# A two-layer graph network on one core: one-hots made in pairs, block transposes on VectorE in the late groups, and h0 remade by ScalarE

## The reference, cut to what matters

```python
h = jnp.maximum(_layernorm(x, axis=-1), 0.0)              # "h0"
# first layer
msg = h[src] + edge_attr_512
msg = msg @ Wm.T + bm
agg = segment_sum(msg, dst, 1250) / jnp.maximum(deg, 1.0)[:, None]
update = jnp.concatenate((h, agg), axis=-1) @ Wu.T + bu
out = h + gelu(update)
x = x + layernorm(out) * gamma + beta
# second layer
h = jnp.maximum(_layernorm(x, axis=-1), 0.0)              # "h1"
rst = (1.0 + eps[0]) * h + segment_sum(h[src], dst, 1250)
h2 = jnp.maximum(rst @ W1 + b1, 0.0) @ W2 + b2
x = x + h2 + h
```

## Time and profile before

| | |
|---|---|
| median of 3 runs | 529.69 us (528.18 to 530.55) |
| the profiled execution | 526.39 us, its span 524.6 us |
| TensorE busy in the span | 482.8 us (92%) |
| VectorE / ScalarE / GpSimd busy | 283.0 / 147.5 / 166.8 us |
| edge loads | 78 of 1024 KB and one of 128 KB, of 98.95 MB moved in all |
| mean granted TensorE clock | 0.992 |

### The profile page before, as it was taken

The page is one execution under the profiler, slowest core; times in us unless marked ns, Lnnn a source line. Parts: engine busy times, 40 slices in busy tenths (PEclk is TensorE's granted clock), DMA queues, the critical chain, the costliest instruction groups (busy, mean ns, idle before and its releaser), DMA issues.

```text
span 524.6 us, 8826 instructions
## 1 busy us (share of the span) xinstructions
PE 482.8 (92%) x3003; PEld 277.0 (53%) x3003; DVE 283.0 (54%) x660; ACT 147.5 (28%) x291; POOL 166.8 (32%) x217
## 2 busy tenths in 40 slices
PE   5889999898898988999999999599989999999997
PEld 4446554444444544675665655379944446744442
DVE  6897887888777779645434789983000000011111
ACT  4416644123222223222237245441011122100000
POOL 7323665333322224000023267636994000000000
PEclk9999999999999999999999999799999999999999
DMA  8998998889999999988820111112040000011111
GB/s 299 316 367 301 338 327 292 348 342 361 352 367 358 374 363 390 408 308 315 271 82 2 32 29 41 35 62 100 1 163 0 0 0 1 0 41 40 41 40 35
DMA packets 31115, 98.95 MB, mean 189 GB/s; under 512 B 3577, under 2 KB 3577, under 8 KB 31067
## 3 DMA queue, kind: packets, MB, share of 16 engines
q1 hardware_dynamic: 30458, 97.27, 50.7%
q10 hardware_dynamic: 608, 1.05, 0.7%
HBM read 95.76 MB, written 2.56 MB: 187 GB/s over the span
## 4 chain that ended last, share of the span: by engine, by line
PE 63%; DVE 21%; issue 6%; PEld 6%; DVEq 1%; POOL 1%; DMA 1%; SPq 0%; PEldq 0%; POOLq 0%
PE ps L1260 13%; PE ps L1245 13%; PE ps L1007 9%; PE ps L1048 7%; DVE A L669 5%; PE ps L1105 5%; PE ps L1106 4%; PE ps L1018 4%; PE ps L1194 3%; PEld ps L1171 3%; PE ps L1036 3%; PEld ps L1172 2%; DVE U L893 2%; DVE tt L871 2%; DVE oneS L648 2%
## 5 line engine op out<-in xcount | busy, mean ns | idle before, releaser
L400 POOL TENSOR_TENSOR aggT<-turned_sums,aggT 128x88 f32 x118 | 53.9, 456 | 107.4 <-ACT turned_sums L473 94.4
L1007 PE MATMUL ps<-ea,oneD 128*22 128x256 f32 x1264 | 83.9, 383 | 1.4 <-DVE oneD L640 0.9
L947 DVE TENSOR_TENSOR U<-ps,U 128x512 f32<-128x512 f32 (+1 forms) x10 | 6.9, 692 | 130.8 <-PE ps L1260 130.8
L467 ACT COPY packed_sums<-ps 128x256 f32<-128x256 f32 x79 | 29.4, 372 | 163.9 <-PE ps L1007 163.9
L1245 PE MATMUL ps<-aggT,W1s 128*128 (+1 forms) x192 | 67.4, 513 | 2.2 <-PEq L1239 2.2
L1260 PE MATMUL ps<-W2s,hid 128*128 128x512 f32 (+1 forms) x160 | 68.8, 592 | 0.0
L669 DVE TENSOR_TENSOR A<-ps,A 128x220 f32 x158 | 60.3, 381 | 8.6 <-PE ps L1018 8.0
L1018 PE MATMUL ps<-oneK,oneS 128*128 128x220 bf16 x316 | 42.5, 259 | 14.7 <-DVE oneS L648 13.0
L1245 PEld LDWEIGHTS ps<-aggT,W1s 128*128 128x128 f32 x192 | 36.4, 190 | 33.1 <-issue 33.0
L1007 PEld LDWEIGHTS ps<-ea,oneD 128*22 128x22 f32 x1264 | 30.5, 101 | 41.1 <-issue 23.6
L648 DVE TENSOR_TENSOR oneK<-iotaP,P_key 128x880 bf16<-128x880 bf16 x79 | 51.8, 655 | 0.0
(11 more groups left out here) (139 smaller groups left out, 645.1 us busy)
## 6 DMA issues: line engine op xcount, KB each, us to landing
ea<-in_edge_attr_dram SPq DMA_DIRECT2D x78, 1024.0 KB, 7.6
X<-in_x_dram SPq DMA_DIRECT2D x1, 2304.0 KB
xt<-in_x_dram SPq DMA_DIRECT2D x9, 256.0 KB, 2.7
out_dram<-U SPq DMA_DIRECT2D x9, 256.0 KB
W1s<-in_L_gnn_W_dram SPq DMA_DIRECT2D x1, 2048.0 KB, 7.7
W2s<-in_L_gnn_W_dram SPq DMA_DIRECT2D x1, 2048.0 KB, 8.7
WuN<-in_L_gnn_Wu_dram ACTq DMA_DIRECT2D x1, 1024.0 KB, 5.4
WuN<-in_L_gnn_Wu_dram SPq DMA_DIRECT2D x1, 1024.0 KB, 6.8
```

The lines of the kernel that those rows point to most:

```text
L400: nc.gpsimd.tensor_tensor(cols, sums, cols, ALU.add).then_inc(early_step, 1)
L1007: last = T.matmul(to.rearrange("p (c d) -> p c d", c=2), oneD[h][:, g * 2 + j, :], data, start=j == 0, stop=j == 1)
```

## The change

In the loop:

1. `oneK` and `oneS` are made for two groups by one instruction (`pair_hots`), with three buffers of two groups; `oneD` has three buffers and is made after the sums of the group before. The half of a group's one-hots that stood between and behind the two adds of `add_counts` is now one instruction between them: keys in even groups, sources in odd ones.
2. `u1(b)` is cut in two: two of its four matmuls in turn U_AT, two in the next.
3. From group 59 on sums are laid out by blocks of 32 columns (16 matmuls of 128 columns for 8 of 256), and VectorE transposes the 32 x 32 blocks straight out of PSUM (`turn_blocks`). The copy by ScalarE and TensorE's two transposes are gone for these 20 groups.
4. The low parts Hl, and the high parts with them, are made from turn 55 on and no longer in turns 6 to 17. A piece waits for its own low part alone.
5. The transposes of h0 stand in other turns, and the ten degree products stand one turn earlier, before `counts`.

In the normalisations: `h0t` is made by ScalarE from the loaded x (`h0_again`), beta is added by VectorE (`add_beta`), and GpSimd keeps the inverse roots alone. The late pieces stand one or two `map_agg` later.

```diff
-HOTS = 2
+HOTS = 3
+SUM_HOTS = 3
+TURNS = 2
...
-    T_AT = [4, 5, 6, 8, 9, 10, 11, 13, 14, 15]
-    U_AT = [7, 12, 16, 21, 26, 32, 37, 42, 47, 52]
-    HH_AT = [t + 2 for t in T_AT]
+    T_AT = [4, 5, 6, 10, 11, 15, 16, 20, 21, 25]
+    U_AT = [7, 12, 17, 22, 27, 32, 37, 42, 47, 52]
+    HH_AT = [FULL - 3 + b for b in range(NT)]
...
-            def ahead(b):
-                pool.wait_ge(xt_in[b % TB], 16 * (b // TB + 1))
-                nc.gpsimd.tensor_tensor(xt[b % TB][:], xt[b % TB][:], betaB[:], ALU.add).then_inc(xb_ready, 1)
-                if b >= TB:
-                    pool.wait_ge(o_sum, b - TB + 1)
-                nc.gpsimd.tensor_tensor(h0t[b % TB][:], Hh[:, b, :].bitcast(F32), Hl[:, b, :].bitcast(F32), ALU.add).then_inc(h0t_ready, 1)
...
+            def h0_again(b):
+                act.wait_ge(xt_in[b % TB], 16 * (b // TB + 1))
+                if b >= TB:
+                    act.wait_ge(o_sum, b - TB + 1)
+                nc.scalar.activation(h0t[b % TB][:], xt[b % TB][:], ACT.Relu, bias=nb0[:, b:b + 1], scale=rs0[:, b:b + 1]).then_inc(h0t_ready, 1)
...
             for k in range(NT + 4):
...
                 for work, lag in ((gelu, 0), (h1, 3), (h1_high, 3), (h1T, 3)):
                     if 0 <= k - lag < NT:
                         work(k - lag)
+                    if work is gelu and k + 1 < NT:
+                        h0_again(k + 1)
...
+            def pair_hots(p, hot, width, name, ready):
+                if p >= HOTS:
+                    dve.wait_ge(counts_done, 2 * (p - HOTS + 1))
...
+                V.tensor_tensor(hot[p % HOTS][:, 0:groups].rearrange("p g h c j -> p (g h) c j"), iota, mine, ALU.is_equal).then_inc(ready, 1)
...
+            def turn_blocks(n):
+                dve.wait_ge(sums_done, n + 1)
+                if n < TURNS + EARLY:
+                    dve.wait_ge(early_step, (n - TURNS + 1) * 2)
+                else:
+                    dve.wait_ge(sum_step, (n - TURNS + 1 - EARLY) * 2)
+                V.transpose(turned_sums[n % TURNS][:], ps[:, n % 2, 0:D // 2]).then_inc(blocks_turned, 1)
...
+            def add_beta(b):
+                dve.wait_ge(h0t_ready, b + 1)
+                V.tensor_tensor(xt[b % TB][:], xt[b % TB][:], betaB[:], ALU.add).then_inc(xb_ready, 1)
...
-            STEPS = [(update, 0), (center, 2), (add_h0, 1), (add_x, 2), (o_moments, 1), (shift, 3), (x1_moments, 2), (o_moments2, 1),
+            STEPS = [(update, 0), (center, 2), (add_h0, 1), (add_x, 2), (o_moments, 1), (shift, 3), (x1_moments, 2), (add_beta, 1), (o_moments2, 1),
                      (x1_moments2, 2), (o_variance, 1), (x1_variance, 2), (low_h1, 4)]
...
+                else:
                     for g in range(2):
-                        for q in range(2):
...
+                        for j in range(2):
+                            data = ea[s][:, g * 2 + j, :].rearrange("p (k q e) -> p q k e", k=FC, q=FC)
+                            for q in range(FC):
+                                to = ps[q * QUAD:q * QUAD + W, n % 2, g * P:(g + 1) * P]
+                                last = T.matmul(to.rearrange("p (k e) -> p k e", k=FC), oneD[h][:, g * 2 + j, :], data[:, q],
+                                                start=j == 0, stop=j == 1)
...
-                late((1, 2, 3, 3, 1)[b])
+                late((0, 0, 2, 3, 3)[b])
```

More of the change, by code:

```diff
@@ L567, in _ @@
             full_conv(0)
+            h0_again(0)
             full_conv(1)
@@ L1209, in _ @@
                 if b == 5:
+                    late(2)
+                    assert not late_pieces
+                transpose_h1(b - 5)
+                if b == 6:
                     pe.wait_ge(agg_done, 2 * FC + 1)
-                transpose_h1(b - 5)
                 if b > 5:
```

217 lines of the change are left out of this document (118 added, 99 removed).

## The result

| | before | after |
|---|---|---|
| median, timed side by side | 528.93 us (527.17 to 530.55) | 520.25 us (520.12 to 522.36) |
| the profiled execution, its span | 526.39, 524.6 us | 520.12, 518.3 us |
| TensorE / VectorE / ScalarE / GpSimd busy | 482.8 / 283.0 / 147.5 / 166.8 us | 481.5 / 280.2 / 147.3 / 147.1 us |
| mean granted TensorE clock | 0.992 | 0.987 |

The ratio is 0.9864, with a 95% interval of 0.9837 to 0.9891: 8.7 us faster, where I forecast 20.3. The spans differ by 6.3 us: the profiled execution before was faster than the timed ones. TensorE's timeline divides them; a stage ends where the next begins.

The account below looks back on a forecast made before the run. TensorE was taken to bound nearly everywhere, VectorE and loads close behind in the loop, VectorE in the normalisations. +1.5 - 10.3 - 2.9 - 8.6 = -20.3 us from the 529.69 median gave 509.4 us, range 501 to 523.

Parts of the forecast that it names:

- two thirds of 15.95 us: Loop: the share of TensorE's idle time expected to go, taken as 10.3 us; the least was nothing.
- Start, +1.5: Before the first counts: wider one-hots for four groups cost 1.4 us, with a little for a third oneD.
- The loop, -10.3: Loop, 58 turns: merged one-hots, freer oneD and split u1 cut TensorE's idle time by 10.3 us.
- rival C: Loop: loads (DMA share 0.94) and VectorE hold it at 2.87 us a turn, 2.3 us go; 517 us, 17%.
- buffers come free more evenly: Loop: with u1 cut in two, TensorE is no longer kept from the sums for four matmuls; no separate size.
- Late turns, -2.9: From group 59 on: dropping TensorE's two transposes saves 3.9 us over twenty turns, less 1.0 us for a collision.
- rivals A and B: Late sums: 32 records keep their pace (524 us, 15%), or short waves also show weight loads (543 us, 5%).
- against this I set 1.0 us: Late turns: GpSimd's low parts meet VectorE's folds while sums wait for VectorE; costs 1.0 us, ends 0 and 4.
- Normalisations, -8.6: Normalisations: TensorE becomes the bound; 7.6 us idle and 2.1 us of half clock go, 1.1 us of waits return.
- two short waits, 1.1 us together: Normalisations, after the last `update`: TensorE catches up with VectorE after two or three blocks; 1.1 us, counted.
- the late pieces only change places with `map_agg`: Normalisations: moving the late pieces later is only a swap of order, with no cost set for it.
- Rival D: Normalisations: `h0_again` waits for x and delays ScalarE's queue, so half of the 8.6 stays; 513.5 us, 12%.

Follow-up runs that it names:

- the run with the two edits together: The changed kernel with low parts made early again and the addition of the last pieces ahead of turn 5: 511.35 us, ratio 0.9698.
- the run with all three: The changed kernel with low parts early, addition of the last pieces ahead of turn 5, and pair one-hots behind both additions: 509.38 us, ratio 0.9644.

## Why the prediction was wrong

**The size was wrong, the direction right.** Of the five stages, the start and the rest came as forecast. Three terms failed. One sum is off as well: two thirds of 15.95 us are 10.6, not 10.3.

*Start, +1.5: right.* +1.8 seen. That the pair one-hots alone do it was not borne out: moving half of them gave 0.4 us back.

*The loop, -10.3: mis-sized, and for the wrong reason.* I rested it on the merged one-hots and took the split of u1 for something that evens out the buffers. The pairs bring 2.3 us. The split brings 10.6, some 3 of it through the clock, and not by buffers: the loads could be halved without effect, so rival C's reason (DMA share 0.94) was no reason either. The failed step is "buffers come free more evenly". What binds, as the waits in the traces read, is the loop between the counts on TensorE and the additions on VectorE, with two banks between them. A burst of 3.6 us stops the counts, VectorE runs dry, and then TensorE waits while VectorE catches up. Two thirds of the idle time was a guess with no mechanism under it; the lists of turns, which I costed at nothing, cost 7.1 us while u1 was whole, 2.9 of it in busy time at half clock. Why they cost that much I did not take apart; in the new lists transposes stand in the turns just before several of the bursts.

*Late turns, -2.9: wrong sign, +2.9.* The gain was sized well, 3.2 us for 3.9. Sums of 32 records last 1.07 us, so rivals A and B fell at once. In a window of 0.04 us of the trace after, from 234.82 us, four of them begin:

```profile
234.82 0.31 PE L1050 MATMUL ps<-ea,oneD 128*22 128x128 f32 x4
```

The Trainium skill (TensorE: Matmul & The Clock Gate, "Wait — 56ns, not 53.3ns?") says that starts never lie closer than about 25 ns. The four lie closer, each in its own group of 32 columns of the array, so here the measurement decides against the rule. The 62 ns per matmul are not seen either: 32 records take 1.07 us. Block transposes take 0.44 us for 0.42. What failed is the term "against this I set 1.0 us" for the collision: it is 6.4 us, with the spell at half clock behind the wait. I had named both parts of it, the ten low parts beside the folds and sums that now wait for VectorE, and even had an upper end of 4. I priced it by the operations' excess and not by the queue: behind folds of 1.8 us also stand oneD and two additions, each of which grows by 0.8 to 1.1 us whatever its own length. A turn of VectorE then takes 7.7 us (205.40 to 213.14) where TensorE needs 3.07, and the sums' bank waits at the end of it. The earlier trace rows held the number: 1.78 - 0.69 = 1.09 us per operation. I used it in the normalisations and not here.

*Normalisations, -8.6: mis-sized, -3.8.* VectorE's turn became what I forecast, and the wait of 5.49 us went. But I wrote that two short waits, 1.1 us together, come back, and looked for them at the end of the pipeline. The one that came is in the middle, 3.3 us, with a spell of 3.4 us at half clock behind it, about 1.7 us more. I had asked what the removed stall uncovers only for `update` and ScalarE, not for the addition that the change itself moved from turn 4 to turn 6, with "the late pieces only change places with `map_agg`". Moved up by one turn, the stage is at 100.58 us, -7.9 against before, close to my 8.6. Rival D's mechanism is in the trace (ScalarE waits 6.4 us for x), but of TensorE's waits only 0.8 us end at ScalarE's h1.

With the low parts early and the addition ahead of turn 5, the kernel takes 511.35 us, and with the one-hots behind both additions 509.38. The 509.4 of the forecast is thus what the change gives without two misplaced steps and with one better placed; the agreement is partly luck, since the loop's terms are others than I wrote and the spells at half clock come and go.

## What to carry to other kernels

Where two engines hand work back and forth through two banks, look at the longest burst of other work on either: cutting it in two can be worth more than making any instruction cheaper, and the busy share of the DMA queues says nothing against it until they are halved in a run. Before you let an engine empty a buffer that another did, count all that stands in its queue ahead of that step, at the slowest rate that a neighbour can impose. And when a stall goes, walk through each step that the change has put one turn later, and ask who waits for it.

## What the runs showed of the hardware that I had not expected

- **A VectorE operation with both inputs in SBUF loses about the same time beside a GpSimd one, whatever its length.** Beside low parts of 1.3 to 1.4 us: oneD 1.32 us for 0.20, an addition of 88 elements 1.33 for 0.25, a fold 1.90 for 0.82, and in the earlier trace rows an add of 512 elements 1.78 for 0.69. The excess is 1.1 us each time (0.8 in the second addition of that turn), near the length of the neighbour's instruction and no share of one's own, so short operations suffer most. The block transposition at 213.14 us, which reads PSUM, takes its 0.44 beside a low part too. The Trainium skill (SBUF — State Buffer, "Who interferes with whom") says that such an instruction contends with a GpSimd one that reads SBUF, and calls the shared ports an exclusive lock. The numbers agree: the excess goes with the number of operations and not with their length, which I could have used for the price.
- **The same work is followed by half clock in one trace and not in another.** Behind the 20 records of the degree products (2.3 us) the granted clock is 0.50 for 3.4 us after the change, so 1.2 GHz, and 0.55 over 3.6 us in the run with early low parts, where TensorE had not waited. In the run with the two edits together they are followed by full clock, and in the run with all three by half clock, with the same late turns. In the trace of before they begin at 228.87 and are followed by full clock:

```profile
224.00:231.00 7.00, 7.00 (x66) 4.80 (x65) 2.17 (x5) 1.78 (x4) 0.00 (x0) 1.00 0.98 365
231.00:238.00 7.00, 7.00 (x58) 4.50 (x58) 2.86 (x12) 1.34 (x4) 0.00 (x0) 1.00 0.70 255
```

- **So with a wait of 2 us.** TensorE waits about 2 us before the first product of the perceptron in each of these traces. Before and after the change the clock stays full behind it and the rest takes 139.52 us; with the addition moved up it falls for 3.4 us and the rest takes 141.20. It is not the addition that decides: in the run with half the loads, which leaves the normalisations as they are, the rest takes 141.08, and in the run with u1 in four pieces, which has the addition moved, 139.52. Each spell costs 1.7 us, and a gain of a few microseconds ahead of one can be partly paid back. What decides it stays open.
